# A two-FFN and time-mixing block in fp32: which products run as three fp32r passes, and where

## The reference

```python
x = x + 0.5 * ffn(layernorm(x))
x = x + attn(layernorm(x))
x = x + 0.5 * ffn(layernorm(x))
# attn:
h = layernorm(x, g1, b1); hh = time_shift(h)
k = (h*tm_k + hh*(1-tm_k)) @ Wk.T          # v with tm_v, Wv; r with tm_r, Wr
rwkv = sigmoid(r) * wkv(decay, first, k, v)  # a scan over 512 tokens
x = x + rwkv @ Wo.T                          # the output product
h = layernorm(x, g2, b2); hh = time_shift(h)
kk = square(relu((h*cm_k + hh*(1-cm_k)) @ Wck.T))   # 1024 keys
x = x + sigmoid((h*cm_r + hh*(1-cm_r)) @ Wcr.T) * (kk @ Wcv.T)
```

## Time and profile before

| | |
|---|---|
| median of 3 runs | 427.72 us |
| the profiled execution | 428.16 us, span 426.3 |
| TensorE busy | 413.4 us, 97% of the span |
| VectorE busy | 369.9 us, 87% |
| ScalarE busy | 338.8 us, 79% |
| GpSimd busy | 181.2 us, 42% |
| granted TensorE clock | 1.00 of full speed |

### The profile page before, as it was taken

One profiled execution on the slowest core, in us unless ns is written; L12 is line 12 of the kernel. 1 busy time (PEld: TensorE's weight loads), 2 busy tenths in 40 slices (PEclk: granted clock), 3 DMA queues, 4 the chain that ended last, 5 costly groups with the idle time before them and its releaser, 6 DMA issues.

```text
span 426.3 us, 6337 instructions
## 1 busy us (share of the span) xinstructions
PE 413.4 (97%) x2038; PEld 333.4 (78%) x2038; DVE 369.9 (87%) x728; ACT 338.8 (79%) x696; POOL 181.2 (42%) x194
## 2 busy tenths in 40 slices
PE   6989989999999999999999999999999999999996
PEld 6765876678868887798769886888779876988895
DVE  2788999998879899998989898989999898979555
ACT  1557978999699979997899879996999479956830
POOL 1536082508272544526381827255462518043011
PEclk9999999999999999999999999999999999999999
DMA  6992010001000011000200020000000000000011
GB/s 200 392 394 78 0 51 0 2 2 50 2 0 0 28 34 41 0 26 1 75 2 17 10 75 1 2 25 27 1 2 25 2 25 0 6 21 27 0 51 50
DMA packets 15971, 18.52 MB, mean 43 GB/s; under 512 B 1082, under 2 KB 13634, under 8 KB 15938
## 3 DMA queue, kind: packets, MB, share of 16 engines
q1 hardware_dynamic: 14538, 17.05, 11.4%
q10 hardware_dynamic: 1400, 1.07, 0.9%
HBM read 13.92 MB, written 4.19 MB: 42 GB/s over the span
## 4 chain that ended last, share of the span: by engine, by line
PE 76%; DVE 7%; issue 1%; POOL 1%; ACT 1%; DVEq 0%; POOLq 0%; ACTq 0%
PE pair L506 20%; PE pair L377 10%; PE pair L389 10%; PE pair L367 7%; PE pair L480 6%; PE pair L484 6%; PE pair L481 6%; PE pair L358 4%; PE pair L450 1%; PE pair L454 1%; PE pair L451 1%; PE pair L527 1%; PE pair L526 1%; PE pair L530 1%; DVE work L1094 1%
## 5 line engine op out<-in xcount | busy, mean ns | idle before, releaser
L506 PE MATMUL pair<-wcv_sb,kk 128*128 128x256 f32 x448 | 100.6, 380 | 0.6 <-ACT kk L775 0.6
L506 PEld LDWEIGHTS pair<-wcv_sb,kk 128*128 128x128 f32 x448 | 83.8, 190 | 12.1 <-ACT kk L775 1.4
L480 PE MATMUL pair<-xck_hi,wck_hi 128*128 128x512 f32 x128 | 54.8, 428 | 0.0
L484 PE MATMUL pair<-xck_lo,wck_hi 128*128 128x512 f32 x128 | 50.7, 396 | 0.0
L481 PE MATMUL pair<-xck_hi,wck_lo 128*128 128x512 f32 x128 | 50.6, 395 | 0.0
L771 ACT ACTIVATE kk<-pair 128x512 f32<-128x512 f32 x64 | 36.4, 590 | 14.2 <-PE pair L484 14.1
L1451 POOL TENSOR_TENSOR x2b<-xs,bias_bc 128x512 f32<-128x512 f32 (+1 forms) x16 | 20.1, 1254 | 54.7 <-DVE xcr L1161 31.9
L775 ACT ACTIVATE kk<-kk 128x512 f32<-128x512 f32 x64 | 36.4, 624 | 0.0
L1495 POOL TENSOR_TENSOR xs<-x,xa 128x512 f32<-128x512 f32 x16 | 20.4, 1274 | 33.7 <-DVE xa L1142 33.7
L1421 POOL TENSOR_SCALAR lowered_x<-sums_x 128x4 f32<-128x4 f32 x12 | 5.0, 417 | 63.2 <-DVE x L1038 57.2
L1451 POOL TENSOR_TENSOR x<-x,bias_bc 128x512 f32<-128x512 f32 x12 | 15.4, 1285 | 37.2 <-DVE xcr_lo L1209 22.3
(11 more groups left out here) (187 smaller groups left out, 1135.3 us busy)
## 6 DMA issues: line engine op xcount, KB each, us to landing
x<-in_x_dram SPq DMA_DIRECT2D x8, 512.0 KB, 4.1
out_dram<-xs SPq DMA_DIRECT2D x15, 256.0 KB, 2.1
xt<-in_xt_dram SPq DMA_DIRECT2D x4, 512.0 KB, 7.9
work<-in_ffn_w_dram ACTq DMA_DIRECT2D x4, 256.0 KB, 5.4
work<-in_ffn_w_dram SPq DMA_DIRECT2D x4, 256.0 KB, 5.4
kk<-in_wck_dram SPq DMA_DIRECT2D x1, 1024.0 KB, 9.6
xs<-in_xt_dram SPq DMA_DIRECT2D x2, 512.0 KB, 10.8
wcv_sb<-in_wcv_dram SPq DMA_DIRECT2D x1, 1024.0 KB, 12.9
```

What stands on the lines that cost most here:

```text
L480: nc.tensor.matmul(key_bank(n), wck_hi[:, h, cols], xck_hi[:, h, :], start=h == 0, stop=False)
L484: last = nc.tensor.matmul(key_bank(n), wck_hi[:, h, cols], xck_lo[:, h, :], start=False, stop=h == CH - 1)
L506: last = nc.tensor.matmul(bank_of("kv", e, i)[:, t % TB * C:(t % TB + 1) * C], kk[:, n, tok:tok + P], wcv_sb[:, n, :], start=n == 0, stop= ...
```

## The change

r and, for f > 0, the output product become three passes; v becomes fp32 in all batches. r's and rwkv's high parts come from ScalarE (`time_gate_input_high`, `output_input_high`), the remainders from VectorE (`time_gate_input_rest`, `output_input_rest`). xr_hi takes the place of xv_hi in `thr`'s storage, rwkv_hi lies in xr's; wo_hi lies over the constants of the setup, which are gathered in one tile `early` for it. In three passes the first two products of a tile no longer wait for the low part. On TensorE the second FFN product of e - 1 moves from behind keys 6, 7 to ahead of them, r behind them, and six instead of four key blocks of tile 0's values come ahead of the output product. ScalarE squares blocks 1 to 5 before rwkv's copies, the gate's tanh goes last. GpSimd's `bias_to_x2(e - 1, 1)` moves from the turn's end to ahead of the attention sums. At the end last_second(0) and last_second(1) come one step later on TensorE, last_add(0) on VectorE too, and the last bias sum is GpSimd's.

The diff's core:

```diff
-    WITHIN = HB // 2
+    WITHIN = HB - 2
...
+        wo_hi, wo_lo = in_place_of("early", "wo_hi", [P, CH, C]), in_place_of("wo_sb", "wo_lo", [P, CH, C])
+        wr_hi, wr_lo = sb("wr_hi", [P, CH, C], F32R), in_place_of("wr_sb", "wr_lo", [P, CH, C])
...
+        rwkv_hi, rwkv_lo = in_place_of("xr", "rwkv_hi", [P, CH, T]), in_place_of("rwkv", "rwkv_lo", [P, CH, T])
+        xr_hi, xr_lo = in_place_of("thr", "xr_hi", [P, CH, T]), in_place_of("xr", "xr_lo", [P, CH, T])
...
+            def three_passes(dst, t, own_hi, own_lo, w_hi, w_lo, low=None):
                 tok = slice(t * P, (t + 1) * P)
                 passes = [(own_hi[:, h, tok], w[:, h, :]) for h in range(CH) for w in (w_hi, w_lo)]
                 passes += [(own_lo[:, h, tok], w_hi[:, h, :]) for h in range(CH)]
                 for j, (own, other) in enumerate(passes):
+                    if low is not None and j == 2 * CH:
+                        pe.wait_ge(*low)
...
             def front_v(f):
+                front("v", f, xv, wv_sb, xv_done, t1_done, vp_ps)
+            def front_r(f):
                 if f == 0:
-                    front("v", f, xv, wv_sb, xv_done, t1_done, vp_ps)
+                    pe.wait_ge(s_bias, 1)
+                    front("r", f, xr, wr_sb, xr_done, thr_done, r_ps)
                     return
                 if f == 1:
-                    pe.wait_ge(s_wv_lo, 1)
+                    pe.wait_ge(s_wr_lo, 1)
                 for o in range(CH):
-                    take(pair_of("v", f), o, t1_done, 2 * f + o + 1)
+                    take(pair_of("r", f), o, thr_done, 2 * f + o + 1)
                     cols = slice(o * P, (o + 1) * P)
                     for h in range(CH):
                         if o == 0:
-                            pe.wait_ge(xv_hi_done, 2 * (f - 1) + h + 1)
-                        nc.tensor.matmul(bank_of("v", f, o), wv_hi[:, h, cols], xv_hi[:, h, :], start=h == 0, stop=False)
-                        nc.tensor.matmul(bank_of("v", f, o), wv_lo[:, h, cols], xv_hi[:, h, :], start=False, stop=False)
+                            pe.wait_ge(xr_hi_done, 2 * (f - 1) + h + 1)
+                        nc.tensor.matmul(bank_of("r", f, o), wr_hi[:, h, cols], xr_hi[:, h, :], start=h == 0, stop=False)
+                        nc.tensor.matmul(bank_of("r", f, o), wr_lo[:, h, cols], xr_hi[:, h, :], start=False, stop=False)
                         if o == 0:
-                            pe.wait_ge(xv_lo_done, 2 * (f - 1) + h + 1)
-                        last = nc.tensor.matmul(bank_of("v", f, o), wv_hi[:, h, cols], xv_lo[:, h, :], start=False, stop=h == CH - 1)
-                    last.then_inc(vp_ps, 1)
-            def front_r(f):
-                if f == 0:
-                    pe.wait_ge(s_bias, 1)
-                front("r", f, xr, wr_sb, xr_done, thr_done, r_ps)
+                            pe.wait_ge(xr_lo_done, 2 * (f - 1) + h + 1)
+                        last = nc.tensor.matmul(bank_of("r", f, o), wr_hi[:, h, cols], xr_lo[:, h, :], start=False, stop=h == CH - 1)
...
             def output_product(f):
                 if f == 0:
                     pe.wait_ge(s_wo, 1)
-                pe.wait_ge(rwkv_done, 2 * f + 2)
-                to_tokens("o", rwkv, wo_sb, xa2_done, f, o_ps)
+                    pe.wait_ge(rwkv_done, 2 * f + 2)
+                    to_tokens("o", rwkv, wo_sb, xa2_done, f, o_ps)
+                    return
+                if f == 1:
+                    pe.wait_ge(s_wo_lo, 1)
+                pe.wait_ge(rwkv_hi_done, 2 * (f - 1) + 2)
+                for i in range(BANKS):
+                    take(pair_of("o", f), i, xa2_done, 2 * f + i + 1)
+                    for t in range(TB):
+                        last = three_passes(bank_of("o", f, i)[:, t * C:(t + 1) * C], i * TB + t, rwkv_hi, rwkv_lo, wo_hi, wo_lo, low=(rwkv_lo_done, 2 * (f - 1) + 2))
...
                 channel_keys(e, (4, 5))
-                if has(f):
+                if e == 0:
                     front_r(f)
+                else:
+                    second_product(e - 1)
                 channel_keys(e, (6, 7))
-                if has(e - 1):
-                    second_product(e - 1)
+                if has(f) and e > 0:
+                    front_r(f)
                 channel_gate(e)
                 if e == LAST:
                     break
-                channel_values(e, 0, range(WITHIN + 2 * (e == 0)))
+                channel_values(e, 0, range(WITHIN))
                 if has(f):
                     output_product(f)
-                channel_values(e, 0, range(WITHIN + 2 * (e == 0), HB))
+                channel_values(e, 0, range(WITHIN, HB))
...
-            last_second(0)
             last_turn(1)
             last_values(2, 3, range(HB // 2, HB))
+            last_second(0)
+            last_turn(2)
             last_second(1)
-            last_turn(2)
             last_second(2)
...
+            def time_gate_input_high(f):
+                for h in range(CH):
+                    act.wait_ge(xr_done, 2 * f + h + 1)
                     if h == 0:
                         act.wait_ge(gated_done, 2 * (f - 1) + 2)
-                    nc.scalar.activation(xv_hi[:, h, :], xv[:, h, :], ACT.Copy).then_inc(xv_hi_done, 1)
+                    nc.scalar.activation(xr_hi[:, h, :], xr[:, h, :], ACT.Copy).then_inc(xr_hi_done, 1)
...
+            def setup_wo_high():
+                act.wait_ge(s_bias_ps, 1)
+                act.wait_ge(s_wo, 1)
+                nc.scalar.activation(wo_hi[:, :, :], wo_sb[:, :, :], ACT.Copy).then_inc(s_wo, 1)
+            def output_input_high(f):
+                act.wait_ge(r_ps, 2 * f + 2)
+                for h in range(CH):
+                    act.wait_ge(rwkv_done, 2 * f + h + 1)
+                    nc.scalar.activation(rwkv_hi[:, h, :], rwkv[:, h, :], ACT.Copy).then_inc(rwkv_hi_done, 1)
...
-                act.wait_ge(vp_ps, 2 * f + 2)
-                for h in range(CH):
-                    act.wait_ge(r_ps, 2 * f + h + 1)
+                act.wait_ge(r_ps, 2 * f + 2)
+                for h in range(CH):
...
-                    value_input_high(f)
                     scaled_difference(f)
...
+                    time_gate_input_high(f)
                     state_exponentials(f, 0)
...
-                    for n in range(3, WITHIN + 2):
+                    for n in range(3, WITHIN):
                         key_square(e, n)
-                    residual_of(f)
-                    for n in range(WITHIN + 2, HB):
+                else:
+                    for n in range(1, WITHIN):
                         key_square(e, n)
-                    channel_gate(e)
-                else:
-                    for n in range(1, HB // 2):
-                        key_square(e, n)
-                    channel_gate(e)
-                    if has(f):
-                        residual_of(f)
-                    for n in range(HB // 2, HB):
-                        key_square(e, n)
+                output_input_high(f)
+                residual_of(f)
+                for n in range(WITHIN, HB):
+                    key_square(e, n)
+                channel_gate(e)
...
+            def output_weight_rest():
+                dve.wait_ge(s_wo, 2)
+                dve.wait_ge(o_ps, BANKS)
+                nc.vector.tensor_tensor(wo_lo[:, :, :], wo_sb[:, :, :], wo_hi[:, :, :].bitcast(F32), ALU.subtract).then_inc(s_wo_lo, 1)
+            def output_input_rest(f):
+                for h in range(CH):
+                    dve.wait_ge(rwkv_hi_done, 2 * (f - 1) + h + 1)
+                    nc.vector.tensor_tensor(rwkv_lo[:, h, :], rwkv[:, h, :], rwkv_hi[:, h, :].bitcast(F32), ALU.subtract).then_inc(rwkv_lo_done, 1)
...
-                    value_input_rest(f)
-                if has(f):
                     wkv_exponents(f)
...
+                    time_gate_input_rest(f)
                 if has(f):
                     wkv_states(f)
...
+                    output_input_rest(f)
                 if has(e - 1):
                     add_second(e - 1, 0)
...
-            last_add(0)
             last_rest(1)
             last_sum(2)
             last_stats(2)
+            last_add(0)
             last_rest(2)
             last_add(1)
-            last_bias(2)
             last_add(2)
...
+                if has(e - 1) and has(f):
+                    pool.wait_ge(o_ps, 2 * f + 1)
+                    bias_to_x2(e - 1, 1)
                 if has(f):
                     attention_sum(f, 0)
                     attention_sum(f, 1)
...
-                if has(e - 1) and e < LAST:
-                    bias_to_x2(e - 1, 1)
...
-                if j < BANKS:
-                    pool.wait_ge(x2_done, 2 * LAST + j + 1)
-                    pool.wait_ge(x3_done, 2 * (LAST - 1) + 2)
-                    add_bias(some_tiles(x2b, j), some_tiles(xs[LAST % XS], j), len(LAST_PARTS[j]), x2b_parts[j])
+                pool.wait_ge(x2_done, 2 * LAST + j + 1)
```

(2 more changed lines are left out.)

59 lines of the change are left out of this document (29 added, 30 removed).

## The result

The changed kernel took 440.38 us (median of 4 runs, 439.13 to 440.96) against 427.68 (427.37 to 428.38) beside it: a ratio of 1.028, 95% interval 1.025 to 1.031. It is slower, 3.6 us beyond the forecast of 436.8 and 0.12 inside the upper end of its range. The profiled execution took 440.07, span 437.7.

The account below looks back on a forecast made before the run. TensorE, 97% busy, was taken as the bound, with VectorE's chain to overtake it. Terms 8.2 + 0.9 - 0.1 + 1.4 - 1.3 = +9.1 on 428.16 gave 437.3, as median 436.8 us; range 431.5 to 440.5.

Parts of the forecast that it names:

- The chain: VectorE, ScalarE and GpSimd from k product to attention-sum turn: normed tile 1.97 later, turns 1 to 5 each 1.65 us longer.
- 0.60 more: GpSimd's bias sum ahead of the attention sums delays the inverse root's start by 0.60 us beyond its wait for the variance.
- A: The start of VectorE's output add, from which the prediction counted GpSimd's steps up to the inverse root.
- A turn of this kind also costs its pipeline's filling ... 0.22: TensorE's turn of the attention sum: 1.43 when held, 1.04 when not; 0.22 us was added for filling.
- Where the output product stands costs nothing: TensorE's output product behind two extra value groups: rwkv_hi ready before it, the remainder meeting the fifth matmul; no cost.
- Turn 0: VectorE's remainders between its scans (+0.24 net), rwkv_hi and rwkv_lo behind, lengthen turn 0 by 0.9 us (0 to 1.5).
- The last turn and the end: Second product ahead of keys 6 and 7 costs 1.4 us; the end's new order brings the last add 1.3 earlier.
- TensorE as the bound: Rival: TensorE doesn't wait at the turn of the attention sum and stays the bound; median 423.3 us, chance 0.13.
- GpSimd isn't late: Rival: the bias sum adds no delay to GpSimd's root, 5 x 0.6 less, 433.8 us; chance 0.18.
- half of it: Rival: the chain is 1.0 us shorter per turn than counted, 431.9 us; chance 0.05.
- no change: Rival: a chain 1.6 us shorter per turn than counted leaves the time the same; chance 0.04.
- not held: VectorE's xr_lo isn't blocked by GpSimd's 2.02 us instruction; the held rival was 5 x 1.4 more, 443.8 us, chance 0.07.

Follow-up runs that it names:

- e1: The changed kernel with only GpSimd's bias sum moved back to the turn's end: 434.02 us, ratio 1.015 to the kernel before.
- e3: The changed kernel with VectorE's add of the second FFN (first half) moved behind the output's add: 433.26 us, ratio 1.013 to the kernel before.
- e2: The changed kernel with the output product in fp32 in all batches, without rwkv_hi and rwkv_lo: 430.38 us, ratio 1.006 to the kernel before.
- e7: The changed kernel with bias sum back, second FFN's add late, and one first-FFN add tile in the rwkv_hi wait: 429.89 us, ratio 1.004 to before.
- e11: The changed kernel with fp32 output product, bias sum at turn's end except turn 6, second add late, last turn's second product back: 429.49 us, ratio 1.004.
- e5: The changed kernel run again unaltered: 439.08 us, ratio 1.026 to the kernel before.
- e8: The changed kernel with the second FFN product behind keys 6 and 7 again in the last turn alone: 436.9 us, ratio 1.019 to the kernel before.
- e9: The kernel before with only the changed kernel's order of the end: 426.46 us, ratio 0.9965 to the kernel before.
- e6: The changed kernel with 6 idle products in TensorE's waits at turn 0's output product and turns 1 to 5's attention-sum turn: 436.9 us, ratio 1.023.

## Why the prediction was right, and where it was off

**The chain.** Right in place and size. From the k product the state scan came at 7.50 (forecast 7.6 at most), rwkv 0.24 earlier (0.3), the wait for rwkv_hi 0.48 (0.65), the output's add 1.54 later (1.55), the root 4.32 behind it (4.3), the normed tile 2.03 later (1.97). A turn lost 1.54 (1.65). Undoing either of the links (e1, e3) gave 0.78 each, taking rwkv's copies away gave 1.15 a turn (e2), and with three links shortened the turn fell below before's (e7). That the total came inside the range is in part luck: the clock took 3.04 us in the profiled execution, no term of the sum or of the range stood for it, and 0.12 more would have been outside.

**"0.60 more" for the bias sum** was 0.78. With the sum ahead the root came at A + 4.32, as forecast (4.3); without it, it comes at A + 3.54 and not 3.65 (e1), and rounding has the rest. The sum also holds VectorE's variance, 0.95 for 0.17, which ends with it and so costs next to nothing. The Trainium skill, SBUF — State Buffer, section Who interferes with whom, says of VectorE's two-port modes and GpSimd that whoever issues first has the shared ports for the whole instruction, and that tensor_scalar can be in such a mode; the variance, a tensor_scalar, ended with GpSimd's sum, and the trace agrees.

**"A turn of this kind also costs its pipeline's filling ... 0.22"** was in part the wrong thing. The 1.43 instead of 1.04 is the third transpose waiting for the last two tiles, 0.39: it stays with TensorE busy up to the turn of xa (e2, e7). The pipeline is the rest: that turn starts 1.96 behind the last value product where it starts 0.22 behind it before the change, 1.74 more, and idle time shows 1.58 of it because matmuls overlap. So 1.74 and 0.39, 2.13, stand for the forecast's 2.07 and 0.22, 2.29: the sum hardly moves.

**"Where the output product stands costs nothing"** held in the changed kernel, where VectorE's chain is the later one. It no longer holds once that chain is shorter: VectorE waits 0.17 for it in e7, 1.03 in e2 and 1.80 in e11, and by the rows of these two it is what makes their turns 0.39 longer than before's.

**Turn 0, "+0.9".** Without its slow stretch it lost 1.21 (e5: 47.11). I counted VectorE's remainders between the scans as 0.24 net; the state scan came 1.07 later, 8.56 after the k product and not 7.49, xr_lo itself taking 1.70. Of this 0.66 was left at rwkv (21.44 for 20.78), because the scan took 1.21 where it had taken 1.63. TensorE waited 1.56 at the output product there (0.15 before, 0.84 with the product in fp32, e2), for which the sum had no term.

**The last turn and the end**, forecast +1.4 and -1.3: +1.57 and -1.24 (e8, e9). Turn 6: -0.34 for -0.1.

**What was missing** is the clock. The sum took 1.00 for granted because the trace of before had it, while it forecast waits of 2 us that the kernel before never had in its turns. Terms without the clock: 7.70 + 1.21 - 0.34 + 1.57 - 1.24 = +8.9, against the forecast +9.1. The profiled run paid 3.04 on top, took 0.28 more behind its last add and 0.89 less at its start: +11.3.

**The rivals.** TensorE as the bound fell: it stood. "GpSimd isn't late" fell with e1, and "half of it" with turns 1.54 longer. The range also left out "no change", so 0.24 and not 0.20 of the chances.

xr_lo was not held in turns 1 to 5 (1.29 for two, at 270.01 above): it started 0.2 before GpSimd's instruction, and that one took 2.90 where it took 2.02. Its second half, which started 0.41 behind GpSimd's, wasn't held either. Turn 0 is different. VectorE, then GpSimd, in the kernel before:

```profile
78.90 1.63 DVE L1094 TENSOR_TENSOR_SCAN work<-work 128x512 f32<-128x512 f32 x1
```

```profile
76.34 3.99 POOL L1488 TENSOR_SCALAR work<-work,lowest 128x512 f32<-128x512 f32 x2
```

and in the changed one:

```profile
76.25 1.28 DVE L1245 TENSOR_TENSOR xcr_lo<-xcr,xcr_hi 128x512 fp32r<-128x512 f32 x2
77.45 1.70 DVE L1236 TENSOR_TENSOR xr_lo<-xr,xr_hi 128x512 fp32r<-128x512 f32 x2
```

```profile
76.43 2.45 POOL L1524 TENSOR_SCALAR work<-work,lowest 128x512 f32<-128x512 f32 x1 [0.28 <-DVE work L1115]
```

Here a VectorE instruction with two operands in SBUF was held by 0.42 each time, the state scan before (1.63 for 1.21) and the first half of xr_lo now (1.10 for 0.68), and GpSimd's took 2.45 for 1.57. So "not held" isn't true of every turn, though it is of those that the sum counts. The same section of the Trainium skill lets the one that starts first have the ports and blocks the other; the trace agrees that GpSimd's, started second, grows, but VectorE's lost 0.42 and not a whole instruction.

## What to carry to other kernels

A cheaper form of a product that needs a split operand puts the split's copy and remainder on the chain that produces that operand; price it there and not on TensorE, which here won 0.63 and then stood 1.58 in each of turns 1 to 5. Independent adds belong into a chain's waits (for a root, for a copy) rather than ahead of them: moving 0.87 us of them was worth 0.78 a turn. Where a forecast has TensorE standing for more than a microsecond, put the chance of its clock falling beside the wait.

## What the hardware showed unexpectedly

- Behind a wait of TensorE of only 1.57 us came a stretch at 1.2 GHz that cost 1.70, in three of three traces at one place, and behind none of the twelve later waits of that length in the same traces; two executions of e8, which has the same waits, show a mean clock of 1.00. With six idle products of 0.223 us in the wait the trace has no such stretch (e6).
- A GpSimd attention sum held a VectorE instruction on four numbers a partition from 0.17 to 0.95; a VectorE remainder that started first stretched GpSimd's from 2.02 to 2.90.
- The start of the program comes in two lengths, first k product at 28.6 to 29.6 or at 31.8 to 32.0, whatever the edit; with medians of four or five runs that hides 0.5 us. In the long ones TensorE waits about 2.5 us for its first normed tile, and the clock fell in three of three.
